# Sums of squares of the queries for two steps at once, finer waits in the last feed-forwards, and new orders in a two-layer decoder

## The reference

```python
x = _layernorm(x + _L0_attn_ref(...))     # causal attention, one head of 256
x = _layernorm(x + _L0_xattn_ref(...))    # long convolution of products with the context, 16 heads
x = _layernorm(x + _L0_ffn_ref(...))      # feed-forward 256 -> 1024 -> 256, ternary weights, 8-bit activations
x = _layernorm(x + _L1_attn_ref(...))     # linear recurrence over the sequence
x = _layernorm(x + _L1_xattn_ref(...))    # cross attention, below
x = _layernorm(x + _L1_ffn_ref(...))      # feed-forward in fp8 with GELU, below

# cross attention: 16 query heads of 128, 4 key heads; hidden 256, 128 rows of x and of context
q = (hidden_states @ Wq + bq).reshape(b, s, NH, HD).transpose(0, 2, 1, 3)
k = (encoder_hidden_states @ Wk + bk) ...; v = (encoder_hidden_states @ Wv + bv) ...
q = _rmsnorm(q, qn_w)                     # by the root of the mean square of 128
k = _rmsnorm(k, kn_w)
scores = jnp.einsum('bhsd,bhed->bhse', q, k) * scale + attention_mask[:, None, :, :]
probs = jax.nn.softmax(scores, axis=-1)
out = jnp.einsum('bhse,bhed->bhsd', probs, v).transpose(0, 2, 1, 3).reshape(b, s, NH * HD) @ Wo

# feed-forward: inputs and weights as fp8, outputs bf16
outputs = _qdot(jax.nn.gelu(_qdot(x, w_gating[0])) * _qdot(x, w_gating[1]), w_linear)
```

## Time and profile before

| | |
|---|---|
| median of 3 runs | 843.54 us (843.42 to 844.71) |
| profiled execution, its span | 842.44 us, 840.4 us |
| TensorE busy | 798.8 us, 95% |
| VectorE busy | 650.6 us, 77% |
| ScalarE busy | 528.8 us, 63% |
| GpSimd busy | 335.6 us, 40% |

### The profile page before, as it was taken

The page is one execution under the profiler, slowest core; times in us unless marked ns, Lnnn a source line. Parts: engine busy times, 40 slices in busy tenths (PEclk is TensorE's granted clock), DMA queues, the critical chain, the costliest instruction groups (busy, mean ns, idle before and its releaser), DMA issues.

```text
span 840.4 us, 13906 instructions
## 1 busy us (share of the span) xinstructions
PE 798.8 (95%) x4610; PEld 613.1 (73%) x4610; DVE 650.6 (77%) x1696; ACT 528.8 (63%) x1315; POOL 335.6 (40%) x419
## 2 busy tenths in 40 slices
PE   6898997899999999999999999999999999999984
PEld 5564666688878777876888768877788778877762
DVE  1778778797989787998878987898888877746553
ACT  3766723763565697448754697359834787669653
POOL 0786875264255214632434233722443142121200
PEclk9999999999999999999999999999999999999997
DMA  8986311001002000200101011000110000000000
GB/s 319 342 259 241 88 64 26 0 14 25 2 34 56 1 1 4 73 0 2 38 14 26 1 64 64 1 1 5 35 51 1 1 23 30 1 13 2 13 1 25
DMA packets 40517, 41.20 MB, mean 49 GB/s; under 512 B 19072, under 2 KB 34944, under 8 KB 40064
## 3 DMA queue, kind: packets, MB, share of 16 engines
q1 hardware_dynamic: 40448, 40.33, 14.9%
HBM read 31.93 MB, written 8.39 MB: 48 GB/s over the span
## 4 chain that ended last, share of the span: by engine, by line
PE 77%; DVE 9%; ACT 8%; issue 3%; POOL 2%; DMA 2%; SPq 0%; POOLq 0%; DVEq 0%; ACTq 0%
PE bank L1371 12%; PE bank L1332 10%; PE bank L1157 6%; PE bank L1350 6%; PE bank L1095 6%; PE bank L1360 5%; PE bank L1292 5%; PE bank L1185 3%; PE bank L1158 3%; PE bank L1225 3%; PE bank L1355 3%; PE bank L1089 2%; PE bank L1338 2%; PE bank L1238 2%; PE bank L1199 1%
## 5 line engine op out<-in xcount | busy, mean ns | idle before, releaser
L1332 PE MATMUL bank<-XTE,w_xq 128*128 128x256 f32 x512 | 122.0, 381 | 2.6 <-ACT QA L716 2.1
L724 ACT ACTIVATE S<-S,mx 128x128 f32<-128x128 f32 x256 | 99.4, 394 | 28.3 <-DVE mx L1026 28.0
L1371 PE MATMUL bank<-w_xo,OX 128*128 128x256 f32 x512 | 115.9, 379 | 0.0
L1332 PEld LDWEIGHTS bank<-XTE,w_xq 128*128 128x128 f32 x512 | 94.4, 190 | 20.4 <-issue 4.4
L1371 PEld LDWEIGHTS bank<-w_xo,OX 128*128 128x128 f32 x512 | 95.2, 190 | 12.2 <-issue 0.2
L1023 DVE SCALAR_TENSOR_TENSOR S<-bank,rq,xmask 128x128 f32<-128x128 f32 x256 | 71.5, 342 | 23.9 <-PE bank L1350 19.9
L715 ACT ACTIVATE QS<-bank,per_partition_sb 128x256 f32<-128x256 f32 x128 | 60.9, 475 | 28.4 <-PE bank L1332 28.2
L1157 PE MATMUL bank<-prod,taps_sb 128*128 128x256 f32 x256 | 77.6, 385 | 0.3 <-DVE Zc L841 0.3
L1350 PEld LDWEIGHTS bank<-KTX,QA 128*128 128x128 f32 x512 | 62.7, 191 | 11.5 <-issue 7.5
L1350 PE MATMUL bank<-KTX,QA 128*128 128x128 f32 x512 | 67.8, 279 | 2.2 <-ACT QA L716 1.7
L310 POOL TENSOR_TENSOR prod<-XTA,ccolA 128x256 f32<-128x256 f32 x96 | 59.1, 648 | 25.4 <-DVE prod L310 14.4
(11 more groups left out here) (231 smaller groups left out, 1749.2 us busy)
## 6 DMA issues: line engine op xcount, KB each, us to landing
keys_spilled<-KTX SPq DMA_DIRECT2D x6, 512.0 KB, 3.4
values_spilled<-VX SPq DMA_DIRECT2D x6, 512.0 KB, 4.4
KTX<-keys_spilled SPq DMA_DIRECT2D x6, 512.0 KB, 3.7
VX<-values_spilled SPq DMA_DIRECT2D x6, 512.0 KB, 4.6
xin<-in_x SPq DMA_DIRECT2D x8, 256.0 KB, 3.0
taps_sb<-in_taps SPq DMA_DIRECT2D x1, 2048.0 KB, 13.5
cnat<-in_ctx SPq DMA_DIRECT2D x8, 256.0 KB, 2.8
ccolA<-in_ctxT SPq DMA_DIRECT2D x32, 64.0 KB, 2.8
```

The lines of the kernel that those rows point to most:

```text
L724: ins = nc.scalar.activation(S[:, b, seq(h)], S[:, b, seq(h)], ACT.Exp, bias=mx[:, b, h:h + 1], accum_out=sm[:, b, h:h + 1])
L1332: ins = nc.tensor.matmul(cols(EQ)[:, h], w_xq[:, k, hh * XDIM:(hh + 1) * XDIM], XTE[:, k], start=k == 0, stop=k == HALVES - 1)
L1371: ins = nc.tensor.matmul(rows(EY)[:, b], OX[:, h, b], w_xo[:, n * XGROUP + h], start=n == 0 and h == 0 and b == 0, stop=n == XKV - 1 and h ...
```

## The change

There are three parts. First, the queries' squares of two steps are kept (`QSs`: `QS` for even steps; for odd steps the weights of the keys, `w_xkv`, which aren't needed once the keys are made), and the sums are taken once for both, behind the odd step: 8 products into the whole of `EQ`, one transpose of 512 columns, one power of 16 columns. The even step's scores are scaled with the same result, so they wait for it too. On TensorE an odd step's first pair of heads waits for ScalarE's copies of the even step, where before every step waited for the transpose of the step before.

Second, the last feed-forwards wait for less: those of groups 5 and 6 for the first and second sum `f_yu` of the one before in place of its norm; that of group 7 transposes into `EQ`, uses the banks `C0`, `C1` for its first part and `A0`, `A1` for its second, and waits for the sum only at the second. In the last group the statistics of the first sequence are taken before the second one's product is there.

Third, the strings of all five engines are new.

```diff
 AHEAD = 4
+LAST_BANKS = (1, 0, 2, 3)
 MADE = (2, 3, 4, 5, 6, 7, 0, 1)
...
         vk, rk = sb("vk", [2, GB * XKV]), sb("rk", [2, GB * XKV])
-        vq, rq = sb("vq", [2, GB * XGROUP]), sb("rq", [2, GB * XGROUP])
-        SSQ = sb("SSQ", [GB * P])
+        vq, rq = sb("vq", [2, 2 * GB * XGROUP]), sb("rq", [2, 2 * GB * XGROUP])
         t = shared("shared_e",
...
         EB = (E0, E1)
+        QSs = QS[:], w_xkv[:, 0].rearrange("p v (h r) -> p (v h) r", r=GB * P)
+        SSQ = w_xkv[:, 1, 0]
         KXs = KX[:], QS[:].rearrange("p (b h) s -> p b (h s)", b=GB)
...
-            return bank[2 * j:2 * j + 2] if g == GROUPS - 1 else bank[0:2]
+            return bank[2 * LAST_BANKS[j]:2 * LAST_BANKS[j] + 2] if g == GROUPS - 1 else bank[0:2]
+        def column(n, b, h):
+            return (n % 2 * GB + b) * XGROUP + h
+        def turned_bank(g):
+            return EQ if g == GROUPS - 1 else A0
...
                 eng.wait_ge(sems["na_out"], nth(min(g + AHEAD - 1, GROUPS - 1), 3, 2))
-                if g > GROUPS - AHEAD:
-                    eng.wait_ge(sems["nf_out"], nth(g - 1))
+                if GROUPS - AHEAD < g < GROUPS - 1:
+                    eng.wait_ge(sems["f_yu"], nth(g - 1, GB, 0))
...
             def queries(g, n):
-                yield
-                gp.wait_ge(sems["e_vq"], nth(g, XKV, n))
-                if g or n >= 2:
+                if n % 2 == 0:
+                    return
+                pair = n // 2
+                yield
+                gp.wait_ge(sems["e_vq"], nth(g, XKV // 2, pair))
+                if g:
                     for b in range(GB):
-                        gp.wait_ge(sems[f"e_mx{b}"], g * XKV + n - 1)
-                sums = SSQ[:].rearrange("p (m r) -> p m r", r=QUARTER)[:, :, 0]
-                sig(inverse_root(rq[:, n % 2], sums, XDIM * 1e-6, vq[:, n % 2]), "e_rq")
+                        gp.wait_ge(sems[f"e_mx{b}"], nth(g - 1, XKV, n))
+                sums = SSQ.rearrange("p (m r) -> p m r", r=QUARTER)[:, :, 0]
+                sig(inverse_root(rq[:, pair], sums, XDIM * 1e-6, vq[:, pair]), "e_rq")
...
                 settled(act)
-                sig(nc.scalar.activation(X8[:], cols(A0), ACT.Copy, saturate=False), "f_x8")
+                sig(nc.scalar.activation(X8[:], cols(turned_bank(g)), ACT.Copy, saturate=False), "f_x8")
                 for j in range(2 * GB):
...
                         q = cols(EQ)[:, h % 2]
-                        nc.scalar.activation(QS[:, h], q, ACT.Square, bias=bq[:, hh:hh + 1])
+                        nc.scalar.activation(QSs[n % 2][:, h], q, ACT.Square, bias=bq[:, hh:hh + 1])
                         ins = nc.scalar.activation(QA[:, n % 2, h], q, ACT.Identity, bias=bq[:, hh:hh + 1])
...
-            def norm(st, src):
+            def norm(st, src, first=0):
                 s = "g" if st == "f" else st
-                for b in range(GB):
+                for b in range(first, GB):
                     ins = nc.vector.bn_stats(stats[s][:, b], src[:, b])
...
                     sig(nc.vector.tensor_tensor(UA[:, b], x[:, b], Y16[:, b], ALU.add), "f_yu")
+                    if g == GROUPS - 1 and b == 0:
+                        dve.wait_ge(sems["f_yu"], nth(g, GB, 0))
+                        nc.vector.bn_stats(stats["g"][:, b], UA[:, b])
                 dve.wait_ge(sems["f_yu"], nth(g, GB, GB - 1))
-                norm("f", UA)
+                norm("f", UA, GB - 1 if g == GROUPS - 1 else 0)
                 yield
...
             def queries(g, n):
-                yield
-                dve.wait_ge(sems["e_ssq"], nth(g, XKV, n))
-                if g or n:
-                    dve.wait_ge(sems["e_rq"], g * XKV + n)
-                sig(nc.vector.transpose(SSQ[:], EQ[:, 0:GB * P]), "e_vq")
+                if n % 2 == 0:
+                    return
+                yield
+                dve.wait_ge(sems["e_ssq"], nth(g, XKV // 2, n // 2))
+                if g or n // 2:
+                    dve.wait_ge(sems["e_rq"], g * (XKV // 2) + n // 2)
+                sig(nc.vector.transpose(SSQ, EQ[:]), "e_vq")
...
                     yield
-                    dve.wait_ge(sems["e_rq"], nth(g, XKV, n))
+                    dve.wait_ge(sems["e_rq"], nth(g, XKV // 2, n // 2))
                     dve.wait_ge(sems[f"e_sc{b}"], nth(g, XKV, n))
                     for h in range(XGROUP):
-                        ins = nc.vector.scalar_tensor_tensor(s3[:, h], EB[b][:, seq(h)], rq[:, n % 2, b * XGROUP + h:b * XGROUP + h + 1],
+                        ins = nc.vector.scalar_tensor_tensor(s3[:, h], EB[b][:, seq(h)], rq[:, n // 2, column(n, b, h):column(n, b, h) + 1],
                                                              xmask[:], ALU.mult, ALU.add)
...
                 pe.wait_ge(sems["ne_out"], nth(g))
-                transpose_rows(X[g % XBUF], A0, "f_xT")
+                transpose_rows(X[g % XBUF], turned_bank(g), "f_xT")
                 for j in range(2 * GB):
...
                     pe.wait_ge(sems["f_x8"], nth(g))
+                    if g > GROUPS - AHEAD and j == (1 if g == GROUPS - 1 else 0):
+                        pe.wait_ge(sems["f_yu"], nth(g - 1, GB, 1))
                     if j >= 1 and g < GROUPS - 1:
...
                     else:
-                        pe.wait_ge(sems["e_vq"], nth(g - 1, XKV, XKV - 1))
+                        pe.wait_ge(sems["e_vq"], nth(g - 1, XKV // 2, XKV // 2 - 1))
                     transpose_rows(X[g % XBUF], EQ, "e_xT")
...
                         pe.wait_ge(sems["e_xTc"], nth(g))
+                    elif n % 2:
+                        pe.wait_ge(sems["e_qc"], nth(g, 2 * XKV, 2 * n - 1))
                     else:
-                        pe.wait_ge(sems["e_vq"], nth(g, XKV, n - 1))
+                        pe.wait_ge(sems["e_vq"], nth(g, XKV // 2, n // 2 - 1))
                     if pr == 0 and (g or n >= 2):
...
                     sig(ins, "e_q")
+                if n % 2 == 0:
+                    return
                 yield
                 pe.wait_ge(sems["e_qc"], nth(g, 2 * XKV, 2 * n + 1))
-                for r in range(P // QUARTER):
-                    part = slice(r * QUARTER, (r + 1) * QUARTER)
-                    ins = nc.tensor.matmul(EQ[part, 0:GB * P].rearrange("p (b h s) -> p b h s", b=GB, h=XGROUP), ones[:, 0:QUARTER],
-                                           QS[:].rearrange("p h (b s) -> p b h s", b=GB)[:, :, :, part], start=True, stop=True)
+                for i in range(2):
+                    for r in range(P // QUARTER):
+                        part = slice(r * QUARTER, (r + 1) * QUARTER)
+                        ins = nc.tensor.matmul(EQ[part, i * GB * P:(i + 1) * GB * P].rearrange("p (b h s) -> p b h s", b=GB, h=XGROUP), ones[:, 0:QUARTER],
+                                               QSs[i].rearrange("p h (b s) -> p b h s", b=GB)[:, :, :, part], start=True, stop=True)
                 sig(ins, "e_ssq")
...
                     if g == GROUPS - 1 and n == XKV - 1:
-                        pe.wait_ge(sems["e_vq"], nth(g, XKV, XKV - 1))
+                        pe.wait_ge(sems["e_vq"], nth(g, XKV // 2, XKV // 2 - 1))
                         keep_clock(EQ, 56)
...
     "pe": (
-        "ssasaakasakkakaasakksakkkkakkkkaakkakakakkskkkkkkkkkckcckckackkaakkakcakcckckkkakkararrarararakaarak"
...
+        "sassaakskakakasakaaasakkkaakaakkkkaskkkkkkkkkkkkckckckakccakkakkackkacckkckkakkakrarrrakrrkaarakaakk"
...
```

45 lines of the change are left out of this document (22 added, 23 removed).

## The result

The changed kernel takes 891.16 us (median of 4 runs, 887.41 to 897.24), the kernel before in the same session 843.48 us (4 runs, 842.18 to 844.71). The ratio is 1.057, with a 95% interval of 1.052 to 1.062: slower, by 47.7 us. The forecast was 843.2 us, with a range of 838.0 to 848.5. The four runs lie 10 us apart, and the profiled one is the fastest of them (887.41): a difference of medians against this kernel is uncertain by about 4 us, and its trace shows some 4 us less than the median.

The account below looks back on a forecast made before the run. TensorE was taken as the bound; 809.66 + 1.8 + 11.0 − 0.7 + 1.0 − 3.4 − 1.5 put the last projection's end at 817.9, giving 842.1 profiled and, 1.1 higher, 843.2 us as median; range 838 to 848.5.

Parts of the forecast that it names:

- rival (b): GpSimd's power delays both steps' scores, four middle pairs lose 1 us each, no middle gain: 848.7 us; chance 0.30.
- The sums: Queries' sums of squares taken in pairs: a double batch holds TensorE about 1.0 us; 3.4 us saved, range 1.6 to 3.8.
- The bare chains of the last group: TensorE's row lacks work to cover the longer chain; waits of 11.0 us before the last projection's end, ends 6 and 14.
- The end: Last transposes start 4.4 us after the last projection's end, not 11.2; full clock gains 1.3, early statistics 0.37.
- The start: New orders at the start: earlier key loads and other moves cancel by slots; 0 us, ends −1 and +2.
- The middle: New orders between 50 and 800 us meet or miss 16.2 us of idleness: −1.5 us, ends −5 and +4.
- wrong in kind: Sign set beforehand: the forecast fails in kind if the stretch 200 to 780 moves over 4 us either way.
- the largest unknown: How new orders between 50 and 800 us meet TensorE's 16.2 us of idleness: −1.5 us, ends −5 and +4.

Follow-up runs that it names:

- the second fitted order with pairs: The changed kernel's code, pairing included, with orders refitted counting VectorE's waits on GpSimd and the half clock behind long idleness: 826.62 us, ratio 0.980.
- the tail alone: The kernel before in its own orders, with only the finer waits, other banks and early statistics of the change's second part: 838.08 us, ratio 0.993.
- the halves: The changed kernel with the 16-column power made as two of 8, the even step's first, each with its own signal: 875.20 us, ratio 1.038.
- the wide one in the old orders: The kernel before with each of its 32 powers made 16 columns wide in place of 8, nothing else changed: 856.51 us, ratio 1.014.
- the trace with the same start: The kernel before with the change's second part and the new start of all five strings, old orders behind it: 849.07 us, ratio 1.007.
- the pairing undone: The changed kernel with sums, transpose and power for each step again, and the queries' letters moved in the strings: 863.13 us, ratio 1.023.
- the short: The changed kernel with the 16-column power replaced by a multiplication of the same operands, leaving out the inverse root: 858.43 us, ratio 1.017.
- the first two fits: Orders fitted to fixed traced durations, for the kernel before with the change's second part (844.48 us) and for the changed kernel's code (846.69 us).
- the first fit: The kernel before with the change's second part, sums for each step, and orders fitted to fixed traced durations: 844.48 us, ratio 1.001.

## Why the prediction was wrong

The step that failed is the one on what hides the longer chain. I wrote that "a longer chain on another engine costs nothing there as long as TensorE's row has other work to run", and counted only TensorE's row between the double batch and the transposes of probabilities. That row did hold enough in most pairs: from the end of the sums to the transposes it has 13.0 us of work in the median of the 16 pairs and 9.6 or more in 13 of them, and TensorE's waits for the probabilities come to 8.7 us in all, 5.7 of them at the first transposes of the last three pairs. What I left out is that VectorE and GpSimd are rows too. While VectorE stands for the power, the norm, the GELU product and the convolution's products behind it stand as well, and TensorE meets them later. I had the place ("GpSimd or VectorE being 2 us behind (both are shared) is enough for it to decide"), as rival (b), but priced it at four pairs and 1 us each. It decides in 14 pairs and gives 32.7 us with the chain's length alone. A question that would have raised the alarm is one line of arithmetic on VectorE's order: 0.7 us of work where 13.3 stood. It shows where VectorE will stand and not what that costs: the second fitted order with pairs has only 2.7 there and loses next to nothing.

Step by step:
- The sums. The power at 2.9 (2.93) and the transpose at 0.8 (0.71) were right. The double batch holds TensorE 1.00 us, as taken:

```profile
599.11 0.64 PE L1363 MATMUL bank<-QS,ones 128*32 128x256 f32 x8
599.56 0.61 PE L1363 MATMUL bank<-w_xkv_sb,ones 128*32 128x256 f32 x8
600.11 1.16 PE L1375 MATMUL bank<-KTX,QA 128*128 128x128 f32 x8
```

 Whether the 3.4 us that follow from it were saved can't be read: no run differs in the sums alone and in nothing else, and with fitted orders the paired kernel is slower by 3.6.
- The bare chains of the last group: mechanism right (1.55 idle for 1.1 and 2.55 for 2.9, at the places named), and the table load and GELUs did stand ahead of the last probabilities' copy.
- The end. 4.4 instead of 11.2, full clock, and 5.8 us for the tail alone: right. The last projection's end was to be 817.9 and is 863.1, as everything ahead of it is late.
- The start, "0 with ends of −1 and +2": 11.0 us by the medians, 6.9 by the profiled executions. I compared TensorE's own slots and the queue of loads, and didn't follow ScalarE's and VectorE's new rows to the first norm. The same mistake as above, at another place.
- The middle, −1.5 with ends −5 and +4: with the last group's chains some 42 us (28.0 and 14.1), where these two were to give 9. From the first queries of group 1 (223 us before) to those of group 7 (740) the lag grows from 15.4 to 31.8, by 16.4 us. With the multiplication in the power's place, and the same orders, it goes from 11.9 to 10.0 there: it was the chain's length that cost the middle. The prediction called itself wrong in kind if the middle moved by more than 4 us, and it was.
- The range. The upper end was built from places I could name. Five strings of several hundred letters were new, and the ends of "the largest unknown" were set as if only TensorE's 16 us of idleness could move.

What stays open: the 14.1 us of the other new orders are measured as a difference only; beside the trace with the same start (old orders behind it) this kernel is some 5 us behind at 340 us, 5 to 7 at 680 and 15 from 740 on, and I made no run for either part. Only half of the 15.2 us between the two spans is idleness of TensorE (52.0 for 44.1 us); the rest is in products that took longer. The numbers that rest on no choice of letters are those of the exchanged powers, which leave all else as it is: 32.7 and 0.35 us for the multiplication, 16.0 for the halves, 12.7 for the wide one in the old orders.

## What to carry to other kernels

When a step on a slow engine gets longer, look at every engine that waits for it in a fixed order, and ask of each what stands between the step's input and its result, and what stands behind the wait. Cover on the engine that bounds the kernel is not enough: whatever stands behind the wait on another engine comes late, and the loss shows where the bound engine next needs it. A wait that has nothing urgent behind it costs nothing. And orders belong to the durations that they were made for: 1.27 us more in each of 32 powers cost 12.7 us with the old orders; the 16 powers of 2.93 us cost 32.7 with the new ones, and 0.35 with orders that knew of them.

## What the hardware showed that I had not expected

VectorE and GpSimd hold each other up in some operations. I counted, in nine traces (the kernel before, the changed one, the tail alone, the pairing undone, the short and the wide root, the root in halves and the first two fits), the VectorE instructions that began while a GpSimd instruction ran. Of 299 that copy or scale more than one column from SBUF to SBUF or take two tensors from SBUF, and began during a multiplication or addition of two tensors on GpSimd, 264 took longer than they otherwise do, each to the end of GpSimd's instruction or beyond. Of some 600 of the same kinds that began during a power none did. Of some 1700 of the other kinds (inputs from PSUM, reductions, statistics) and of 179 that scale a single column, begun during a multiplication or addition, none did either. So a product of 128x4 took 1.53 us for 0.16, and in the first fit VectorE was busy 25 us longer (674.8 for 650.0) with the same instructions. The Trainium skill, "GPSIMD Engine Reference", 1. Specifications, says that GpSimd shares its SBUF interfaces with VectorE, in contention with its two-port modes and with operations on two SBUF inputs; the traces agree for instructions with two SBUF inputs (136 of 147 took longer), and add that a power that is running holds nothing up. The power itself can be held: of 109 powers that began while VectorE worked on two SBUF inputs, 91 took longer, as this one of the kernel before, 2.14 us for 1.67:

```profile
378.72 1.28 DVE L887 TENSOR_TENSOR UG<-X,g 128x512 f32<-128x512 f32 x2
378.77 2.14 POOL L456 TENSOR_TENSOR rq<-vq,minus_half 128x8 f32<-128x8 f32 x1
```

TensorE's clock was at half for 3.4 us at the wait of 3.67 us that ended at 128.5 in the first fit and at that of 2.04 us at 391.5 in the kernel with the wide root; behind two waits of 1.66 us (144.0 and 147.7 in the kernel before) it stayed at full. But the length of one wait does not decide it. In the second fit with pairs the clock was at half for 3.4 us from 159.1 on, behind waits of 0.97 and 0.47 us and at one of 0.33:

```profile
157.00 0.41 PE L1146 MATMUL bank<-ident,S 128*128 128x128 f32 x2 [0.97 <-ACT S L620]
157.88 1.13 PE L1151 MATMUL bank<-V,PT 128*128 128x256 f32 x4 [0.47 <-ACT PT L624]
```
